# Third staging buffer, finer waits, and a router moved into the normalisation, in an eight-core transformer layer

## The chip, the cores and the metric

The kernel runs on 8 cores of one Trainium2 chip. All cores run one program; each computes 1024 tokens of one of two sequences of 4096, and reads 256 more on either side for the attention window (EXT = 1536 tokens). The cores don't exchange data. The metric is the device time of the slowest core, in microseconds (us).

## The reference, cut to what matters

```python
x = x + 0.5 * ffn(layernorm(x))          # x: (2, 4096, 4096) f32
x = x + attn(layernorm(x))
x = x + 0.5 * ffn(layernorm(x))

def ffn(x):                               # W_base 4096x4096, 8 experts of rank 16, top 2
    logits = x @ W_router.T
    p, idx = top_k(softmax(logits), 2); p = p / p.sum()
    combine = sum over k of p[k] * one_hot(idx[k])
    h = einsum('nd,erd->ner', x, A) * combine[:, :, None]
    return x @ W_base.T + b_base + 2 * einsum('ner,eor->no', h, B)

def attn(x):                              # 32 query heads of 128, one key and value head
    Q, K, V = x @ Wq.T, x @ Wk.T, x @ Wv.T
    Q, K = rope(Q), rope(K)
    for i in range(0, S, 256):            # windows of 512, half overlapping
        a = sigmoid(Q[i:i+512] @ K[i:i+512].T * scale); a = a / a.sum(-1)
        w = a @ V[i:i+512]
        out = linear blend of the former window's w and this one
    return out @ Wo.T
```

## The kernel before

Activations stand feature by token: `xlnb` holds the normalised input, 32 feature chunks x 1536 tokens, in bf16. Everything else on chip lives in one SBUF tensor, `arena`, carved up anew for each stage, so the profile names nearly every tile `arena`. The order of work is written out by hand: `Prog.emit` appends an instruction to one engine's list with the semaphore counts that it waits for, and each engine runs its list in order. All loads of weights and small tables go through SyncE's (SP's) queue, all loads and stores of activations through GpSimd's (POOL's).

Three stages follow each other: `ffn` on 1536 tokens, `attn`, `ffn` on 1024 tokens.

**`ln_prep` (lines 184 to 249)** opens each stage. Per chunk of 128 tokens it loads 2 MB in two DMAs into one of two buffers, casts and squares them on ScalarE (L207, L208), sums over features with 32 matmuls (L214), derives mean and inverse deviation on one partition on VectorE, with a square root on ScalarE (L231), spreads them by two matmuls (L237, L239), and applies them with two VectorE passes (L241, L245). The load of chunk i waits for the apply of chunk i-2.

**`ffn`.** After `ln_prep`, for each 512 tokens (three times in the first `ffn`, twice in the second) come 32 matmuls with the adapters' A (L325), 32 with the router (L331), a copy of the logits (L335), transposes (L340), the gates of the two best experts on VectorE and ScalarE (L343 to L381), four transposes back (L385), a copy (L388) and the product of gates and A's result (L391). I call this the router phase. Then the loop over 32 output chunks `of`: four slices of W_base (8 x 128 columns, 512 KB) are loaded and cast, and for each 512 tokens 32 matmuls (L422) and the adapters' B (L425) are done, evicted and stored.

**`make_stager` (lines 251 to 267)** loads and casts all weights. A load goes into one of two f32 buffers of `wstage` and waits for the cast that last read this buffer; ScalarE casts it to bf16 (L263). The DMA instruction itself is always line 47.

**`attn`.** Eight slices of Wk and eight of Wv (256 KB each) are staged, then K and V computed. While the first group of heads runs, POOL copies x1 to x2 in HBM in 64 pieces (the precopy). 32 heads run in four groups of eight (`hp`, and `hh` within one). `stage_wq(h)` stages eight slices of Wq. `feed(k)` issues the next k of the 64 matmuls of the coming head's Q projection (L576), 32 for each half of the tokens. Per head: rope on VectorE (L593 to L600), then ScalarE's list gets the eight casts for head h+1, then five windows, each with two score matmuls (L616), `feed(6)`, a sigmoid (L626), two more score matmuls (L631), `feed(6)`, a sigmoid (L637), the product with V (L646), `feed(4)`, and the blend by diagonal matrices (L653 to L681). A group's last head stages nothing. A group's first Q projection is issued as a whole, `feed(64)`, behind its own eight casts. After each group the Wo phase runs 32 turns of two staged slices of Wo, 2 x 8 matmuls (L708), two evictions on ScalarE (L716) and two DMAs that add to x2 in HBM (L45); an eviction waits until the adding DMA two before has landed.

The wait at the heart of `feed`, before:

```python
if j == 0:
    w = [("scalar", wqc[h]), ("vector", prep_v)] + list(extra_first)
```

`wqc[h]` is ScalarE's count after all eight casts.

Of the kernel before, what the change touches and what calls it, by code (L numbers as in the profile page):

```python
# [89 lines left out]
def build():  # L90
# [177 lines left out]
    def ffn(src_r, dst_r, ntok):  # L268
# [20 lines left out]
        prep_v, prep_t = pd["vector"], pd["tensor"]
        a = Arena(arena_t, PREP_B)  # L290
        wstage = [a.f32(8 * 128, (8, 128)), a.f32(8 * 128, (8, 128))]
        wb = [a.bf16(NIF * 128, (NIF, 128)), a.bf16(NIF * 128, (NIF, 128))]
        sl_sizes = []
        t0 = 0
        while t0 < ntok:
            n = min(512, ntok - t0)
            sl_sizes.append((t0, n))
            t0 += n
        slabs = [[a.f32(n) for (s0, n) in sl_sizes] for _ in range(2)]
        gxb = a.f32(512)  # L300
        lg = arena_t[0:8, a.alloc(512) + 0:a.off]
        ltm = a.f32(32, (4, 8))
        gate = a.f32(32, (4, 8))
        eq1 = a.f32(32, (4, 8))
        eq2 = a.f32(32, (4, 8))
        mskb = a.f32(32)
        m1c = a.f32(4)
        m2c = a.f32(4)
        p1c = a.f32(4)
        p2c = a.f32(4)  # L310
        stage = make_stager(wstage)
# [2 lines left out]
        hw_cnt = 0
        hw_hist = [0] * (NTS + 2)
        se_prev = 0
        sg_prev = 0
# [511 lines left out]
```

How the kernel before makes its waits and increments, by code:

```python
            def run(eng):  # L738
                hw = {}
                for fn, waits, inc, isem in pr.ops[e]:
                    for (we, wv) in waits:
                        if we == e:
                            continue
                        if wv > 0 and hw.get(we, -1) < wv:
                            eng.wait_ge(sems[we], wv)
                            hw[we] = wv
                    ins = fn(eng)
                    if inc:
                        ins.then_inc(sems[isem], inc)
                if e == "gpsimd":
                    for s, v in total_st.items():
                        if v:
                            eng.wait_ge(sems[s], v)
```

## Time and profile before

| what | us |
|---|---|
| median of 2 runs | 5023.42 (5001.85 to 5044.99) |
| the profiled execution | 4825.5 |
| its span, slowest core (core 3) | 4824.0 |
| spans of the eight cores | 4787.1 to 4824.0 |
| granted TensorE clock, eight cores | 0.818 to 0.825 |
| busy PE / DVE / ACT / POOL | 3083.9 / 994.4 / 1313.3 / 533.5 |

The profile is of one execution, on its slowest core. PE is TensorE's matmuls and PEld its weight loads, DVE is VectorE, ACT ScalarE, POOL GpSimd, SP SyncE. A row of the timeline gives the start and the length of an instruction (or of several in a row, "x32") and in brackets how long its engine was idle before it and what ended that. PEclk is the clock granted to TensorE as a share of 2.4 GHz; its two levels are 0.5 (1.2 GHz) and 1.0. The stages lie in the span as follows: first `ffn` to 1063 us (router phases from 289.7), normalisation of `attn` to 1312, K and V to 1414, the four groups of heads with their Wo phases to 4083, second `ffn` to the end.

### The profile page before, as it was taken

What the parts mean: (1) busy time and instruction counts of PE and PEld (TensorE: products, weight loads), DVE (VectorE), ACT (ScalarE), POOL (GpSimd) and SP (SyncE); (2) the same over time, 40 slices, a digit from 0 to 9 for tenths busy, and PEclk for the clock granted to TensorE, in tenths of its full rate; (3) what the DMA queues carried; (4) which work ended last, traced back from release to release, by engine and by line L of the source; (5) the groups of instructions that cost most, each with busy time, mean ns of one, the idle gap of its engine ahead of it and who ended that gap; (6) DMA issues with size and microseconds to landing.
All of it is one profiled execution on the core that took longest, in us unless ns stands there. A gap on an engine that the chain in (4) does not pass through costs nothing.

```text
span 4824.0 us, 40133 instructions; the slowest of 8 cores (4787.1 to 4824.0 us)
## 1 busy us (share of the span) xinstructions
PE 3083.9 (64%) x14804; PEld 1474.6 (31%) x14804; DVE 994.4 (21%) x1698; ACT 1313.3 (27%) x1657; POOL 533.5 (11%) x772
## 2 busy tenths in 40 slices
PE   1359999983265555656656566556566565249998
PEld 1224444432123332223332233322233322124443
DVE  2531111115512220012220022200122200441111
ACT  3322211213312222322223322223222232423222
POOL 0101111111011101200002100012000021101111
PEclk8679999996677777877868788878888687569999
DMA  4415556553343324741117711148411177327776
GB/s 107 119 36 159 172 167 178 170 150 101 104 137 111 111 81 92 141 91 44 35 32 143 142 49 36 35 83 147 94 43 35 30 143 155 106 57 206 218 211 182
DMA packets 647219, 537.33 MB, mean 111 GB/s; under 512 B 33905, under 2 KB 566642, under 8 KB 646770
## 3 DMA queue, kind: packets, MB, share of 16 engines
q1 hardware_dynamic: 556914, 283.07, 22.1%
q0 software_dynamic: 90112, 251.71, 21.8%
q8 instruction: 119, 1.95, 0.2%
q14 instruction: 74, 0.61, 0.1%
HBM read 408.85 MB, written 125.83 MB: 111 GB/s over the span
## 4 chain that ended last, share of the span: by engine, by line
PE 44%; DMA 27%; DVE 11%; ACT 10%; issue 5%; DVEq 1%; POOL 1%; SPq 1%; ACTq 0%; POOLq 0%
PE PS L422 14%; PE PS L576 9%; DMA arena<-wqT 6%; DMA x2h<-arena 6%; PE PS L708 5%; DMA arena<-woT 5%; DMA arena<-x2h 5%; ACT arena L263 4%; PE PS L646 3%; DMA out<-arena 3%; PE PS L673 2%; PE PS L631 2%; DVE arena L653 2%; DVE arena L664 2%; PE PS L677 2%
## 5 line engine op out<-in xcount | busy, mean ns | idle before, releaser
L422 PE MATMUL PS<-arena 128*128 128x512 bf16 x5120 | 1137.4, 380 | 25.5 <-ACT arena L263 18.9
L263 ACT ACTIVATE arena<-arena 128x512 bf16<-128x512 f32 (+1 forms) x784 | 582.8, 765 | 1173.6 <-PE PS L425 455.2
L708 PE MATMUL PS<-arena 128*128 128x512 bf16 x2048 | 585.7, 450 | 349.8 <-ACT arena L263 349.8
L576 PE MATMUL PS<-arena 128*128 128x512 bf16 x2048 | 560.4, 415 | 306.9 <-ACT arena L263 306.9
L422 PEld LDWEIGHTS PS<-arena 128*128 128x128 bf16 x5120 | 502.1, 98 | 635.3 <-issue 36.3
L45 POOL DMA_DIRECT2D x2h<-arena x256 | 217.2, 849 | 2108.9 <-ACT arena L716 1854.8
L708 PEld LDWEIGHTS PS<-arena 128*128 128x128 bf16 x2048 | 220.0, 111 | 714.8 <-issue 572.9
L576 PEld LDWEIGHTS PS<-arena 128*128 128x128 bf16 x2048 | 207.7, 105 | 562.3 <-issue 384.6
L653 DVE COPY arena<-PS 128x516 f32<-128x516 f32 (+1 forms) x160 | 94.2, 589 | 1155.8 <-PE PS L646 1155.8
L716 ACT ACTIVATE arena<-PS 128x512 f32<-128x512 f32 x256 | 152.9, 597 | 647.3 <-PE PS L708 441.3
L673 PE MATMUL PS<-arena 128*128 128x128 f32 x512 | 133.4, 350 | 231.2 <-DVE arena L668 231.2
L214 PE MATMUL PSM<-arena 128*1 128x256 bf16 x512 | 90.1, 358 | 288.3 <-ACT arena L208 288.3
L429 DVE TENSOR_SCALAR arena<-arena 128x512 f32<-128x512 f32 x160 | 77.1, 482 | 785.1 <-DMA arena<-xin 411.8
L681 ACT ACTIVATE arena<-PS 128x256 bf16<-128x256 f32 x128 | 49.2, 384 | 662.6 <-PE PS L677 662.6
L593 DVE TENSOR_TENSOR arena<-PS,arena 128x1024 f32<-128x1024 f32 x32 | 39.0, 1219 | 833.6 <-PE PS L576 833.6
L646 PE MATMUL PS<-arena 128*128 128x130 bf16 x2048 | 159.8, 234 | 48.1 <-ACT arena L637 45.8
L637 ACT ACTIVATE arena<-PS 128x1024 bf16<-128x1024 f32 (+1 forms) x160 | 136.6, 854 | 189.1 <-PE PS L631 189.1
L673 PEld LDWEIGHTS PS<-arena 128*128 128x128 f32 x512 | 97.2, 237 | 278.9 <-issue 278.9
L626 ACT ACTIVATE arena<-PS 128x1024 bf16<-128x1024 f32 (+1 forms) x160 | 135.9, 850 | 137.1 <-PE PS L616 134.4
L646 PEld LDWEIGHTS PS<-arena 128*128 128x128 bf16 x2048 | 135.9, 104 | 116.4 <-issue 111.2
L207 ACT ACTIVATE arena<-arena 128x4096 bf16<-128x4096 f32 x32 | 115.7, 3615 | 190.4 <-DMA arena<-x1h 92.7
L616 PE MATMUL PS<-arena 128*128 128x512 bf16 (+1 forms) x320 | 95.8, 388 | 102.7 <-DVE arena L600 102.7
(95 smaller groups left out, 2216.3 us busy)
## 6 DMA issues: line engine op xcount, KB each, us to landing
arena<-wbaseT SPq DMA_DIRECT2D x256, 512.0 KB, 5.7
x2h<-arena POOLq DMA_DIRECT2D x320, 256.0 KB, 4.6
arena<-wqT SPq DMA_DIRECT2D x256, 256.0 KB, 2.9
arena<-woT SPq DMA_DIRECT2D x256, 256.0 KB, 5.4
arena<-xin POOLq DMA_DIRECT2D x24, 1024.0 KB, 10.2
arena<-xin POOLq DMA_DIRECT2D x96, 256.0 KB, 3.9
x1h<-arena POOLq DMA_DIRECT2D x96, 256.0 KB, 2.3
arena<-x1h POOLq DMA_DIRECT2D x24, 1024.0 KB, 9.7
```

Of the source, the lines that this page charges most:

```text
L45: fn = lambda q, o=out, i=in_: q.dma_start(out=o, in_=i, accum_op=ALU.add)
L207: pr.emit("scalar", lambda s, p=par: s.activation(xb[p][:, :, 0:128], xf[p], ACT.Copy), wsc, 1)
L263: c = pr.emit("scalar", lambda s, si=i % 2, d=dst_bf_ap: s.activation(d, wstage[si], ACT.Copy), wc, 1)
L422: pr.emit("tensor", lambda t, c=c, sl=slot, of=of, t0=t0, n=n: t.matmul(sl, wb[of % 2][:, c, :], xlnb[:, c, t0:t0 + n], start=(c == 0), st ...
L576: qmm[h] = pr.emit("tensor", lambda t, c=c, par=h % 2, hf=hf: t.matmul(PS1[:, hf * 512:(hf + 1) * 512], wqb[par][:, c, :], xlnb[:, c, 256 ...
L626: pr.emit("scalar", lambda s, qn=qn, sp=sp: s.activation(sgb[sp][:, 0:2, 0:qn], PS2[:].rearrange("p (c t) -> p c t", c=2)[:, :, 0:qn], ACT ...
L637: sig_cnt = pr.emit("scalar", lambda s, qn=qn, sp=sp: s.activation(sgb[sp][:, 2:4, 0:qn], PS2[:].rearrange("p (c t) -> p c t", c=2)[:, :, ...
L646: avm = pr.emit("tensor", lambda t, p=p, kc=kc, kc0=kc0, st=st, sp_=sp_, sp=sp: t.matmul(PS3[:, p * 256:p * 256 + 130], sgb[sp][:, kc, p * ...
L653: wn_last = pr.emit("vector", lambda v, npp=npp, wi=wi: v.tensor_copy(wnr[wi % 2][:, 0:npp, :], PS3v[:, 0:npp, 0:129]), [("tensor", avm)], 1)
L673: pr.emit("tensor", lambda t, b=b, j=j, sA=sA: t.matmul(PS4[:, j * 128:(j + 1) * 128], wnr[b % 2][:, sA + j, 0:128], diag[:, j, :], start= ...
L708: mmc = pr.emit("tensor", lambda t, gg=gg, of=of, ts2=ts2, sl=slot: t.matmul(sl[:, 0:512], wqb[of % 2][:, gg, :], wout8[:, gg, ts2 * 512:( ...
L716: ev = pr.emit("scalar", lambda s, sli=sli, sl=slot: s.activation(slabs[sli], sl[:, 0:512], ACT.Copy), [("tensor", mmc), (xsem, pr.cnt[xse ...
```

## The change

Three edits. `make_stager` takes as many buffers as it is given, and is given three in `ffn` and in `attn`; the third has a DMA semaphore of its own. `feed` no longer waits for all eight casts at its first matmul: in the first half of the tokens, each fourth matmul waits for the cast of the slice that it and the next three read. The router phase of `ffn` becomes a function, `aphase`, called from a hook inside `ln_prep` after every fourth chunk's apply, on the 512 tokens that are then normalised. Its PSUM results move to halves of PS1 and PS2 that `ln_prep` doesn't use, and its small tiles to a place before `ln_prep`'s buffers.

```diff
-    def ln_prep(src_r, ntok, base, entry=()):
+    def ln_prep(src_r, ntok, base, entry=(), hook=None):
...
+            if hook is not None:
+                hook(i, apply2)
...
     def make_stager(wstage):
+        nb = len(wstage)
...
-            if i - 2 in state["cast"]:
-                wdma.append(("scalar", state["cast"][i - 2]))
-            sem = "wload%d" % (i % 2)
-            g = pr.dma(sem, wstage[i % 2], src_ap, wdma)
+            if i - nb in state["cast"]:
+                wdma.append(("scalar", state["cast"][i - nb]))
+            sem = "wload%d" % (i % nb)
+            g = pr.dma(sem, wstage[i % nb], src_ap, wdma)
...
-        pd = ln_prep(src_r, ntok, PREP_B, snap1)
...
-        for ts in range(NTS):
+        def aphase(ts, wait_v):
...
-            wmm = [("vector", prep_v)]
+            wmm = [("vector", wait_v), ("scalar", sm_cast)]
...
+        def hook(i, ap2):
+            if i % 4 == 3 and (i // 4) < NTS:
+                aphase(i // 4, ap2[i])
+
+        pd = ln_prep(src_r, ntok, OFL_B, snap1, hook=hook)
...
+        wstage = [a.f32(8 * 128, (8, 128)) for _ in range(3)]
...
-        wstage = [a.f32(4 * 128, (4, 128)), a.f32(4 * 128, (4, 128))]
+        wstage = [a.f32(4 * 128, (4, 128)) for _ in range(3)]
...
         def stage_wq(h, extra=()):
+            subs = []
...
-                stage(wqT_r[:, s8 * 4:(s8 + 1) * 4, h * 128:(h + 1) * 128],
-                      wqb[h % 2][:, s8 * 4:(s8 + 1) * 4, :], (), ew)
+                subs.append(stage(wqT_r[:, s8 * 4:(s8 + 1) * 4, h * 128:(h + 1) * 128],
+                            wqb[h % 2][:, s8 * 4:(s8 + 1) * 4, :], (), ew))
+            wq_sub[h] = subs
...
                     w = []
+                    if hf == 0 and c % 4 == 0:
+                        w.append(("scalar", wq_sub[h][c // 4]))
                     if j == 0:
-                        w = [("scalar", wqc[h]), ("vector", prep_v)] + list(extra_first)
+                        w += [("vector", prep_v)] + list(extra_first)
```

On ScalarE, in the normalisation of the first `ffn`, around the end of chunk 3, the order before is this (L231 is the square root of chunk 3, L207 and L208 cast and square chunk 4, then chunk 5):

```order
L231 ACTIVATE arena<-arena 1x128
L207 ACTIVATE arena<-arena 128x32x128
L208 ACTIVATE arena<-arena 128x32x128
L231 ACTIVATE arena<-arena 1x128
L207 ACTIVATE arena<-arena 128x32x128
```

Now at the same place (L325 is the copy of the logits, L335 that of the transposed logits, L350 and L353 the sigmoids, four pairs of them, L380 the copy of the gates; in the changed file):

```order
L231 ACTIVATE arena<-arena 1x128
L325 ACTIVATE arena<-PS 8x512
L335 ACTIVATE arena<-PS 128x32
L350 ACTIVATE arena<-arena 128x1
L353 ACTIVATE arena<-arena 128x1
...
L380 ACTIVATE arena<-PS 128x512
L207 ACTIVATE arena<-arena 128x32x128
L208 ACTIVATE arena<-arena 128x32x128
L231 ACTIVATE arena<-arena 1x128
```

The whole router phase stands between chunk 3's square root and chunk 4's cast. The same holds on TensorE and VectorE, after chunks 3, 7 and 11 of the first `ffn` and 3 and 7 of the second; the last hook is where the router's last phase stood before.

In `attn` no instruction changes its place; waits do. TensorE's list in window 0 of head 0, before (L616 and L631 are score matmuls, L576 the Q matmuls of the next head, L646 the product with V):

```order
L616 MATMUL PS<-arena 128x256 [waits s_vector]
L616 MATMUL PS<-arena 128x256
L576 MATMUL PS<-arena 128x512 [waits s_scalar]
L576 MATMUL PS<-arena 128x512 x5
L631 MATMUL PS<-arena 128x256 [waits s_scalar]
L631 MATMUL PS<-arena 128x256
L576 MATMUL PS<-arena 128x512 x6
```

And now (L634 and L649 are the score matmuls, L594 the Q matmuls, in the changed file):

```order
L634 MATMUL PS<-arena 128x256 [waits s_vector]
L634 MATMUL PS<-arena 128x256
L594 MATMUL PS<-arena 128x512 [waits s_scalar]
L594 MATMUL PS<-arena 128x512 x3
L594 MATMUL PS<-arena 128x512 [waits s_scalar]
L594 MATMUL PS<-arena 128x512
L649 MATMUL PS<-arena 128x256 [waits s_scalar]
L649 MATMUL PS<-arena 128x256
L594 MATMUL PS<-arena 128x512 x6
```

One wait for eight casts has become a wait for the first cast and, four matmuls later, one for the second; the later casts need no wait of their own here, since L649 waits for a sigmoid that stands behind all of them on ScalarE.

## Rows read from the trace of the kernel before

**Rows 1.** The page: its first line, and the chain that ended last, by line.
```profile
span 4824.0 us, 40133 instructions; the slowest of 8 cores (4787.1 to 4824.0 us)
...
PE PS L422 14%; PE PS L576 9%; DMA arena<-wqT 6%; DMA x2h<-arena 6%; PE PS L708 5%; DMA arena<-woT 5%; DMA arena<-x2h 5%; ACT arena L263 4%; PE PS L646 3%; DMA out<-arena 3%; PE PS L673 2%; PE PS L631 2%; DVE arena L653 2%; DVE arena L664 2%; PE PS L677 2%
```

**Rows 2.** Groups and waits of the whole span: us in total, times, longest us.
```profile
L263 ACT ACTIVATE arena<-arena 128x512 bf16<-128x512 f32 (+1 forms) x784 | 582.8, 765 | 1173.6 <-PE PS L425 455.2 <-DMA arena<-wbaseT 396.0 <-DMA arena<-wqT 277.5
...
PE PS L576 <- ACT arena L263: 306.9, 28, 17.3
...
ACT arena L716 <- DMA x2h<-arena: 206.0, 82, 4.3
```

**Rows 3.** Windows: length; busy PE, PEld, DVE, ACT, POOL; PEclk, DMA share, GB/s.
```profile
375.00:1063.00 688.00, 686.67 (x3168) 310.47 (x3166) 106.77 (x191) 127.72 (x124) 101.39 (x188) 1.00 0.58 167
1312.00:1352.00 40.00, 0.58 (x2) 0.28 (x3) 0.00 (x0) 10.07 (x16) 5.51 (x11) 0.50 0.71 216
1850.00:2084.00 234.00, 146.26 (x512) 54.81 (x510) 0.00 (x0) 70.62 (x126) 53.46 (x63) 0.85 0.76 142
2164.09:2181.16 17.07, 7.21 (x28) 2.97 (x29) 0.50 (x2) 4.86 (x8) 0.00 (x0) 0.54 0.40 115
2181.16:2189.46 8.30, 6.65 (x45) 3.62 (x44) 2.09 (x7) 2.05 (x2) 0.00 (x0) 1.00 0.00 0
```

**Rows 4.** Timeline, head 9: start us, us, instruction [idle before]; ScalarE, then TensorE.
```profile
2161.55 1.14 ACT L263 ACTIVATE arena<-arena 128x512 bf16<-128x512 f32 x2
...
2170.17 0.63 ACT L263 ACTIVATE arena<-arena 128x512 bf16<-128x512 f32 x1 [0.68 <-DMA arena<-wqT]
...
2173.76 0.63 ACT L263 ACTIVATE arena<-arena 128x512 bf16<-128x512 f32 x1 [0.68 <-DMA arena<-wqT]
...
2174.53 2.72 PE L576 MATMUL PS<-arena 128*128 128x512 bf16 x6 [9.86 <-ACT arena L263]
2177.05 0.63 PE L631 MATMUL PS<-arena 128*128 128x256 bf16 x2
```

**Rows 5.** Waits from 1430 to 1850 us, the first group of heads.
```profile
PE PS L576 <- ACT arena L263: 68.5, 6, 11.8
```

**Rows 6.** Timeline of ScalarE, head 2, beside the precopy.
```profile
1537.66 0.63 ACT L263 ACTIVATE arena<-arena 128x512 bf16<-128x512 f32 x1 [1.13 <-DMA arena<-wqT]
...
1541.60 0.63 ACT L263 ACTIVATE arena<-arena 128x512 bf16<-128x512 f32 x1 [1.57 <-DMA arena<-wqT]
```

**Rows 7.** Timeline, first head of the second group: ScalarE, then TensorE.
```profile
2084.34 1.14 ACT L263 ACTIVATE arena<-arena 128x512 bf16<-128x512 f32 x2
...
2094.67 0.63 ACT L263 ACTIVATE arena<-arena 128x512 bf16<-128x512 f32 x1 [1.43 <-DMA arena<-wqT]
...
2098.12 0.63 ACT L263 ACTIVATE arena<-arena 128x512 bf16<-128x512 f32 x1 [1.24 <-DMA arena<-wqT]
...
2098.89 16.75 PE L576 MATMUL PS<-arena 128*128 128x512 bf16 x64 [17.28 <-ACT arena L263]
```

**Rows 8.** Timeline, normalisation, chunks 3 to 5: VectorE, then ScalarE.
```profile
128.58 4.42 DVE L245 TENSOR_TENSOR arena<-arena,PS 128x4096 bf16<-128x4096 f32 x1
...
129.32 3.62 ACT L207 ACTIVATE arena<-arena 128x4096 bf16<-128x4096 f32 x1 [7.60 <-DMA arena<-xin]
...
144.56 0.31 ACT L231 ACTIVATE arena<-arena 1x128 f32<-1x128 f32 x1 [8.11 <-DVE arena L230]
145.74 3.62 ACT L207 ACTIVATE arena<-arena 128x4096 bf16<-128x4096 f32 x1 [0.87 <-DMA arena<-xin]
```

**Rows 9.** Timeline, the three router phases: TensorE, then ScalarE.
```profile
289.71 9.90 PE L325 MATMUL PS<-arena 128*128 128x512 bf16 x32 [9.19 <-DVE arena L245]
...
309.78 1.28 ACT L358 ACT_TABLE_LOAD   x1 [1.67 <-DVE arena L355]
...
316.92 0.60 ACT L388 ACTIVATE arena<-PS 128x512 f32<-128x512 f32 x1 [4.25 <-PE PS L385]
...
365.11 0.60 ACT L388 ACTIVATE arena<-PS 128x512 f32<-128x512 f32 x1 [4.25 <-PE PS L385]
```

More of the change, by code:

```diff
@@ L287, in ffn @@
         snap1 = [("scalar", sm_cast), ("vector", pr.cnt["vector"]), ("tensor", pr.cnt["tensor"])]
-        pd = ln_prep(src_r, ntok, PREP_B, snap1)
[L289 to L311, printed above, removed]
-        NTS = ntok // 512
[L314 to L317, printed above, removed]
-        for ts in range(NTS):
+        ga = Arena(arena_t, PREP_B)
+        gxb = ga.f32(512)
+        lg = arena_t[0:8, ga.alloc(512) + 0:ga.off]
+        ltm = ga.f32(32, (4, 8))
+        gate = ga.f32(32, (4, 8))
+        eq1 = ga.f32(32, (4, 8))
+        eq2 = ga.f32(32, (4, 8))
+        mskb = ga.f32(32)
+        m1c = ga.f32(4)
+        m2c = ga.f32(4)
+        p1c = ga.f32(4)
+        p2c = ga.f32(4)
+        OFL_B = ga.off
+        NTS = ntok // 512
+        st_aph = {"hw": 0, "hw_hist": [0] * (NTS + 2), "se": 0, "sg": 0}
+        def aphase(ts, wait_v):
             cols = slice(ts * 512, (ts + 1) * 512)
             hslot = PS3[:, (ts % 2) * 512:(ts % 2) * 512 + 512]
-            wmm = [("vector", prep_v)]
+            wmm = [("vector", wait_v), ("scalar", sm_cast)]
             if ts >= 2:
-                wmm.append(("vector", hw_hist[ts - 2]))
+                wmm.append(("vector", st_aph["hw_hist"][ts - 2]))
             for c in range(NIF):
@@ L331, in ffn @@
                 h_cnt = pr.emit("tensor", lambda t, c=c, cc=cols: t.matmul(
[L332 removed]
+                    PS1[0:8, 512:1024], rb16[:, c, :], xlnb[:, c, cc],
                     start=(c == 0), stop=(c == NIF - 1)), wrt if c == 0 else [],
                     1 if c == NIF - 1 else 0)
[L335 removed]
+            se = pr.emit("scalar", lambda s: s.activation(lg, PS1[0:8, 512:1024], ACT.Copy),
                          [("tensor", h_cnt)], 1)
[L337 removed]
+            st_aph["se"] = se
             tp = 0
@@ L385, in ffn @@
                 tg = pr.emit("tensor", lambda t, qc=qc: t.transpose(
-                    PS4[:, qc * 128:(qc + 1) * 128], gxb[:, qc * 128:(qc + 1) * 128], id32),
+                    PS2[:, 512 + qc * 128:512 + (qc + 1) * 128], gxb[:, qc * 128:(qc + 1) * 128], id32),
                     [("vector", vgx), ("scalar", se2)] if qc == 0 else [], 1 if qc == 3 else 0)
-            sg = pr.emit("scalar", lambda s: s.activation(gxb, PS4[:, 0:512], ACT.Copy),
+            sg = pr.emit("scalar", lambda s: s.activation(gxb, PS2[:, 512:1024], ACT.Copy),
                          [("tensor", tg)], 1)
-            sg_prev = sg
-            hw_hist[ts] = hw_cnt = pr.emit("vector", lambda v, h=hslot, cc=cols: v.tensor_tensor(
-                hwb[:, cc], h, gxb, ALU.mult), [("scalar", sg)], 1)
+            st_aph["sg"] = sg
+            st_aph["hw_hist"][ts] = st_aph["hw"] = pr.emit(
+                "vector", lambda v, h=hslot, cc=cols: v.tensor_tensor(
+                    hwb[:, cc], h, gxb, ALU.mult), [("scalar", sg)], 1)
+        def hook(i, ap2):
+            if i % 4 == 3 and (i // 4) < NTS:
+                aphase(i // 4, ap2[i])
+        pd = ln_prep(src_r, ntok, OFL_B, snap1, hook=hook)
+        prep_v, prep_t = pd["vector"], pd["tensor"]
+        hw_cnt = st_aph["hw"]
+        a = Arena(arena_t, OFL_B)
+        wstage = [a.f32(8 * 128, (8, 128)) for _ in range(3)]
+        wb = [a.bf16(NIF * 128, (NIF, 128)), a.bf16(NIF * 128, (NIF, 128))]
+        sl_sizes = []
+        t0 = 0
+        while t0 < ntok:
+            n = min(512, ntok - t0)
+            sl_sizes.append((t0, n))
+            t0 += n
+        slabs = [[a.f32(n) for (s0, n) in sl_sizes] for _ in range(2)]
+        stage = make_stager(wstage)
         grp_cnt = {}
@@ L546, in attn @@
         dg_guard = 0
+        wq_sub = {}
         def stage_wq(h, extra=()):
+            subs = []
             for s8 in range(8):
```

17 lines of the change are left out of this document (8 added, 9 removed).

## The prediction

> **What bounds the kernel now.** I read the page's chain of waits first [rows 1]. No engine owns it: TensorE's two large products (L422, the feed-forward; L576, the Q projection) lead, and then come loads of weights (wqT, woT) and stores. So each stage has its own limit, and I read them one at a time.
>
> The waits and groups show where engines stand still [rows 2]. TensorE waits 306.9 us, in 28 pieces, ahead of L576, for ScalarE's L263, the cast of a weight slice from f32 to bf16. L263 itself waits 277.5 us for wqT, 396.0 for wbaseT and 455.2 for TensorE. These three are 1128.7 of its 1173.6 us, which leaves 45 us for all other loads: woT costs hardly any wait. In the Wo stretches the evictions L716 wait for accumulating stores instead (206.0 us).
>
> The windows give the limits [rows 3]. The first feed-forward's product loop, 375 to 1063 us, has TensorE busy 686.67 of 688 us at full clock: a third staging buffer gives nothing there. The K/V staging (1312 to 1352) has TensorE idle, the DMA engines 0.71 busy. In the Wo phase (1850 to 2084) they are 0.76 busy. In one head of the attention, 17.07 us lie between the first score matmul of window 0 and that of window 1, at a mean clock of 0.54, half level (1.2 GHz) nearly throughout; the next window takes 8.30 us at full level (2.4 GHz).
>
> The cause is in the timeline of that head [rows 4]. ScalarE casts eight slices for the next head before its first sigmoid: two at once, then each as its load lands, from 2161.55 to 2174.39 us, 12.8 us for 8 x 0.63 = 5.0 us of work. With two buffers a load starts only when the cast two before is done. TensorE stands still for 9.86 us, because the first L576 matmul waits for all eight casts, and its six matmuls of 0.427 us then stand before L631. The counts [rows 5] say six such stops in the first group of heads, so 24 in four groups; the other four of the 28 are at the groups' first heads.
>
> **The change part by part, against the profiled execution (4825.5 us, its span 4824.0).**
>
> *Third buffer in the heads.* The load of slice i now waits for cast i-3. Casts 0 to 2 run at once, and the loads that fed casts 2 to 5 at present now feed 3 to 6 at the same times; one more, triggered by cast 2, joins them. So cast 7 comes about where cast 5 stands today, 2170.17 instead of 2173.76: 3.6 us [rows 4]. In the first group of heads, where a precopy shares the DMA engines, it is 1541.60 - 1537.66 = 3.9 us [rows 6]. Bounds: nothing, if three loads in flight land no sooner than two; and 7.8 us, if all waits between casts go (12.8 - 5.0).
>
> *The Q matmuls wait by quarter-slices.* The first six need casts 0 and 1 alone, so they run while ScalarE still casts. Today they occupy TensorE from 2174.53, and L631 starts at 2177.05 [rows 4]. It would otherwise start when the sigmoid has ended, some 0.8 us after 2174.30, so 2.0 us go. Against that, window 1 is reached sooner after TensorE's restart and may begin at the lower level: between 0 and 0.8 us, I take 0.4. Per head: 3.6 + 2.0 - 0.4 = 5.2, and 5.5 in the first group. Heads: 18 x 5.2 + 6 x 5.5 = 126.6 us.
>
> *First head of each group.* Today 64 matmuls wait for eight casts: casts from 2084.34 to 2098.75, matmuls from 2098.89 for 16.75 us, to 2115.64 [rows 7]. By the same rule cast 7 comes at 2094.67 and ends at 2095.30; 28 matmuls are done by then, and 36 x 0.216 = 7.8 us remain: 2103.1, so 12.5 us earlier. If TensorE stayed at 1.2 GHz for all 64 (27.3 us from 2085.2) only 3.1 us would be won; with matmuls queued nearly all the time I take 12.5. Four times: 50.0.
>
> *K and V staging.* Sixteen slices in the 40 us of that window. The DMA engines' own work is 0.71 x 40 = 28.4, so at most 11 us can go, at least none. I take 8, nearer the upper end, since each cast there waits for a load.
>
> *Wo phases.* Loads of woT are issued at the same casts as today and are already hidden [rows 2]: 0. *Feed-forward loops:* 0, as read above; at their start three slices instead of two are there when the gates end, which saves one step from landing to landing. Two such steps are 3.6 us in rows 4, so I take 1.8, between none and 3.6: 3.6 together.
>
> *The router moved into the normalisation.* This one costs. The hook puts 64 matmuls and the gate chain behind chunks 3, 7 (and 11), on every engine in program order, ScalarE's included. Chunk 4's L207 today starts at 129.32, 3.7 us before chunk 3 is applied (128.58 + 4.42 = 133.00) [rows 8]. Now it stands behind the gate copy, which in today's first phase ends 27.8 us after the phase's first matmul begins (289.71 to 316.92 + 0.60 [rows 9]), 28.0 with the semaphore behind the apply: 31.7 us late. Chunk 5 follows behind chunk 4's square root (144.56 + 0.31 - 129.32 = 15.6 us later) and a table load of 1.3 us [rows 9], at 44.9 instead of 12.7 after the apply (145.74 - 133.00): 32.2 late. Chunk 7 hangs on chunk 5, through the buffer. So a hook in the middle costs 32.2 us, three times (two in the first feed-forward, one in the second): 96.6. At the end one phase is left where there were three, and two: a later phase costs (365.11 - 316.92) / 2 = 24.1 us [rows 9], three times 72.3. Net +24.3 us. Its loads on POOL and SP wait for the applies as before, so only order counts. Bounds: -72 if the hooks were hidden wholly, +97 if the end gave nothing back.
>
> The load of the sigmoid table takes 1.28 us [rows 9], and six more changes of table come in, all counted above. The Trainium skill (ScalarE: Activation LUTs, "What ACT_TABLE_LOAD costs") gives 2.66 us for a change, with a drain; the row shows 1.28, and no run here shows the rest. By the page the sum would be 8 us worse.
>
> Sum: -126.6 - 50.0 - 8.0 - 3.6 + 24.3 = -163.9 us, that is 4661.6 in the profiled execution, 3.4% less. The median of the two runs shown, 5023.42, is 4.1% above the profiled one (factor 1.041), for a reason that the profile does not show. I scale with it: -170.6, 4853 us.
>
> **The rivals.**
>
> *TensorE wakes earlier.* Window 0 runs at a mean clock of 0.54, window 1 at 1.00 [rows 3]. If the matmuls run during the casts bring the full level forward, the rest of window 0 is some 2.0 us shorter and the 0.4 is not lost: 24 x 2.4 = 57.6 more; 163.9 + 57.6 = 221.5, x 1.041 = 231, 4793 us. For it: the idle piece of 9.86 us [rows 4] shrinks by the cast gain and the 2.6 us of the six matmuls, to under 4. Against: only six matmuls are let in. The Trainium skill (TensorE: Matmul & The Clock Gate, "HAM oscillation — how this bites in real kernels") says that a product interrupted by waits for its next slice falls to half clock each time, and that this goes when the waits go. The 0.54 agrees with the first half; the second would give this rival.
>
> *Three loads land no sooner.* Then the casts stay as they are; only the quarter waits gain: 24 x 1.6 = 38.4 in heads, at a group's first head 2098.75 + 7.8 = 2106.6, so 9.1 x 4 = 36.4, less 24.3: 50.5, x 1.041 = 52.6, 4971 us. Against: the DMA engines are 0.40 busy in that stretch [rows 3], so a third load in flight has room.
>
> *Slower: the accumulating stores.* The Wo phase has 4 x 32 = 128 turns, each bound in part by a landing [rows 2], with the DMA engines 0.76 busy [rows 3]. If deeper staging delays each landing by x, it costs 128 x: from 1.28 us on the whole gain is gone. At 2.2 us it is 281.6 - 163.9 = +117.7, x 1.041, 5146 us. Against: the same loads are issued at the same casts.
>
> *The hook does hide the router,* as its place suggests. Then -72.3 instead of +24.3: 163.9 + 96.6 = 260.5, x 1.041 = 271, 4752 us. Against: ScalarE's order, above.
>
> **How the numbers follow.** Forecast 4853: 0.54. Earlier clock 4793: 0.23. No sooner 4971: 0.12. Slower: 0.04. Hidden router: 0.04. The rest, 0.03, are sums of small misses. A measurement here tells 2% from nothing: faster by more than that is below 4923. Forecast, clock, hidden router and some of the rest give 0.84 faster, 0.12 same, 0.04 slower. The range is 4650 to 4930. Its low end takes in the sum against the profiled execution itself (4662), should the runs of the changed kernel lie there; its high end holds the forecast with the bad ends of K/V, first heads and feed-forward starts (8 + 38 + 4), and a margin for a quarter of the cast gain in the heads. It leaves out the two cases above.
>
> **What would show it.** Right: between score matmuls of windows 0 and 1 some 11.5 instead of 17.07 us; the wait L576 for casts down from 306.9 to under 120; wqT's waits at least a third less; first head's Q matmuls end some 19 us after the casts began, not 31; chunk 4's L207 some 28 us after chunk 3's apply instead of 3.7 before it; six more table loads; Wo phases unchanged near 233 us. Wrong: the eighth cast still 12 us after the first; that L207 within 10 us of the apply; Wo phases longer by over 10 us each; or a window 1 at half clock.

## The result and the profile after

The changed kernel takes 0.9717 of the time of the kernel before, with a 95% interval of 0.9689 to 0.9745: 2.8% faster, where the forecast's sum was 3.4%. Its profiled execution took 4678.3 us, and the median of its 11 runs is 4702.99 us. Runs of both kernels lie near the profiled time or some 4% above it, and the ratio compares the near ones alone; the factor 1.041 in the forecast of 4853 us came from two runs that were both of the far ones. The range, 4650 to 4930, holds the median.

The page's first line and its chain by line:

```profile
span 4676.8 us, 40189 instructions; the slowest of 8 cores (4646.6 to 4676.8 us)
...
PE PS L434 24%; DMA x2h<-arena 8%; PE PS L594 8%; PE PS L726 6%; DMA arena<-wqT 4%; ACT arena L266 4%; PE PS L664 3%; DMA arena<-woT 3%; PE PS L691 2%; PE PS L649 2%; DVE arena L671 2%; ACT arena L207 2%; ACT arena L208 2%; DVE arena L682 2%; PE PS L695 2%
```

The chain of [rows 1] had wqT at 6% and the Q matmuls (L576, now L594) at 9%; they are down to 4% and 8%. The product loop (L422, now L434) leads by more than before, 24%. Groups, table loads and waits of the whole span (us in total, times, longest us):

```profile
L266 ACT ACTIVATE arena<-arena 128x512 bf16<-128x512 f32 (+1 forms) x784 | 567.5, 762 | 1052.1 <-PE PS L437 612.3 <-DMA arena<-wbaseT 232.9 <-DMA arena<-wqT 168.8
...
L594 PE MATMUL PS<-arena 128*128 128x512 bf16 x2048 | 579.3, 425 | 18.1 <-ACT arena L266 16.9 <-DVE arena L533 1.1
...
L350 ACT ACT_TABLE_LOAD x5 | 6.4, 1283 | 8.3 <-DVE arena L347 8.3
L231 ACT ACT_TABLE_LOAD x5 | 6.4, 1283 | 38.6 <-DVE arena L230 38.6
...
ACT arena L734 <- DMA x2h<-arena: 222.4, 92, 4.5
...
PE PS L649 <- ACT arena L644: 157.9, 73, 7.0
```

Against [rows 2], TensorE's wait for casts ahead of the Q matmuls went from 306.9 to 16.9 us, and ScalarE's wait for wqT from 277.5 to 168.8. Part of it moved: the second pair of score matmuls (L649, before L631) now waits 157.9 us for the first sigmoid, where it waited 47.1 before (below), since in window 0 no Q matmuls cover that wait any longer. Together the two waits fell from 354.0 to 174.8 us. From the kernel before:

```profile
PE PS L631 <- ACT arena L626: 47.1, 49, 1.3
```

The wait of the Wo evictions for accumulating stores stays (222.4, before 206.0). There are ten table loads at L231 and L350, six more than before.

Windows, columns as in [rows 3]:

```profile
387.98:1074.00 686.02, 686.02 (x3167) 310.41 (x3168) 106.07 (x190) 124.45 (x124) 101.39 (x188) 1.00 0.56 167
1327.00:1361.00 34.00, 0.00 (x0) 0.00 (x0) 0.00 (x0) 10.07 (x16) 4.36 (x8) 0.50 0.84 234
1813.46:2050.00 236.54, 148.61 (x512) 55.59 (x512) 0.00 (x0) 70.29 (x127) 53.46 (x63) 0.84 0.77 140
2165.59:2178.30 12.71, 8.59 (x29) 3.67 (x30) 0.60 (x2) 4.23 (x7) 0.00 (x0) 0.50 0.51 146
2178.30:2186.60 8.30, 6.66 (x46) 3.62 (x45) 1.99 (x6) 2.05 (x2) 0.00 (x0) 1.00 0.00 0
```

The product loop is unchanged, 686 us at full clock. K/V staging has the DMA engines 0.84 busy instead of 0.71. One Wo phase: 236.5 us, 0.77 busy. Window 0 of head 10 takes 12.71 us, where head 9 took 17.07 before, and all of it at the lower level, 0.50. Over 24 heads the mean went from 16.8 to 12.5 us. Window 1 runs at the full level, 8.30 us at 1.00, as before. The timeline of that head, ScalarE, then TensorE:

```profile
2162.58 1.66 ACT L266 ACTIVATE arena<-arena 128x512 bf16<-128x512 f32 x3
...
2171.60 0.63 ACT L266 ACTIVATE arena<-arena 128x512 bf16<-128x512 f32 x1 [0.93 <-DMA arena<-wqT]
2172.14 0.58 ACT L644 ACTIVATE arena<-PS 128x512 bf16<-128x512 f32 x1
...
2165.97 2.76 PE L594 MATMUL PS<-arena 128*128 128x512 bf16 x6
2172.86 0.59 PE L649 MATMUL PS<-arena 128*128 128x256 bf16 x2 [4.12 <-ACT arena L644]
2173.24 2.77 PE L594 MATMUL PS<-arena 128*128 128x512 bf16 x6
2175.80 1.08 PE L664 MATMUL PS<-arena 128*128 128x130 bf16 x8
2176.66 1.80 PE L594 MATMUL PS<-arena 128*128 128x512 bf16 x4
2178.30 0.60 PE L634 MATMUL PS<-arena 128*128 128x512 bf16 x2
```

Three casts at once and the last at 2171.60 us: 9.65 us from first to last, not 12.8 [rows 4]. Six Q matmuls run in that time. TensorE then idles until 2172.86, and everything behind it runs at half clock: six Q matmuls at 0.427 us each, the product with V (L664, 1.08 us for 8), four more in 1.80 us. Before, the same stretch read as follows (TensorE, head 9, behind the last of [rows 4]):

```profile
2177.48 2.53 PE L576 MATMUL PS<-arena 128*128 128x512 bf16 x6
2179.84 0.62 PE L646 MATMUL PS<-arena 128*128 128x130 bf16 x8
2180.30 1.02 PE L576 MATMUL PS<-arena 128*128 128x512 bf16 x4
```

There TensorE restarted with the first six Q matmuls at 2174.53, and at 2179.84 the full level was back, while window 0 still ran: L646 took 0.62 us and the four 1.02. Here it restarts only with L649 at 2172.86, nearer to the end of window 0 (2178.30), and the full level comes with window 1. So in these two heads 1.08 - 0.62 + 1.80 - 1.02 = 1.24 us of the gain are given back.

The first head of the second group, ScalarE, then TensorE:

```profile
2049.89 1.66 ACT L266 ACTIVATE arena<-arena 128x512 bf16<-128x512 f32 x3
...
2063.93 0.63 ACT L266 ACTIVATE arena<-arena 128x512 bf16<-128x512 f32 x1 [1.35 <-DMA arena<-wqT]
...
2061.29 7.93 PE L594 MATMUL PS<-arena 128*128 128x512 bf16 x36 [0.78 <-ACT arena L266]
```

The casts run from 2049.89 to 2064.56, the matmuls between them; the last 36 matmuls go in 7.93 us, at full clock, and end at 2069.22, 19.3 us after the first cast began, where [rows 7] show 31.3.

The normalisation around the first hook (VectorE, ScalarE, and VectorE again, chunk 7):

```profile
127.36 4.42 DVE L245 TENSOR_TENSOR arena<-arena,PS 128x4096 bf16<-128x4096 f32 x1
...
158.81 0.60 ACT L380 ACTIVATE arena<-PS 128x512 f32<-128x512 f32 x1 [4.24 <-PE PS L377]
159.30 3.61 ACT L207 ACTIVATE arena<-arena 128x4096 bf16<-128x4096 f32 x1
...
174.49 1.28 ACT L231 ACT_TABLE_LOAD   x1 [8.07 <-DVE arena L230]
175.78 0.31 ACT L231 ACTIVATE arena<-arena 1x128 f32<-1x128 f32 x1
...
239.54 4.42 DVE L245 TENSOR_TENSOR arena<-arena,PS 128x4096 bf16<-128x4096 f32 x1
```

Chunk 4's L207 starts at 159.30, 27.5 us after chunk 3's apply ended (131.78), where [rows 8] had it 3.7 us before. Directly ahead of it stands L380, the gate copy. Then a table load. Chunk 7's apply ends 112.2 us after chunk 3's.

### Where the time went

All eight cores run one program without exchange, so I cut each core's trace at the same instructions and took the median over eight cores. The heads are counted from one rope's first instruction to the next's; the 24 are those that hold a cast row before window 0. In us, and beside it the same for the experiments below. A few matmul records of cores 0 and 6 are missing, so the stretches are cut by time and not by counting. Not listed are the first product loop (685.3 and 686.2) and small stretches, and medians don't add exactly, so the columns don't add up to the span. e1 is its first trace. The router's delay is the last row but one: the time from chunk 3's apply to chunk 7's.

| stretch | before | after | e1 | e2 | e3 | e4 | e5 | e6 | e8 | e9 | e10 |
|---|---|---|---|---|---|---|---|---|---|---|---|
| 24 heads | 1246.5 | 1148.2 | 1146.9 | 1155.4 | 1239.1 | 1257.3 | 987.2 | 1145.0 | 984.1 | 1099.4 | 985.4 |
| last eviction to rope, 3 groups | 94.9 | 60.2 | 61.3 | 84.3 | 72.5 | 94.1 | 61.3 | 61.1 | 60.3 | 61.0 | 61.9 |
| first K matmul to first rope | 78.5 | 66.4 | 66.2 | 74.5 | 72.3 | 78.3 | 65.6 | 65.8 | 66.1 | 65.7 | 65.2 |
| K/V staging | 41.0 | 34.4 | 34.7 | 34.5 | 41.8 | 41.8 | 34.7 | 34.4 | 34.5 | 34.6 | 34.5 |
| first opening, to first product matmul | 371.7 | 384.9 | 368.3 | 365.5 | 366.6 | 386.4 | 369.2 | 322.7 | 322.2 | 385.6 | 323.9 |
| second opening | 261.3 | 269.7 | 258.2 | 258.8 | 260.8 | 269.1 | 259.1 | 241.7 | 241.6 | 266.4 | 243.0 |
| Wo phases, 4 | 928.8 | 932.7 | 934.7 | 934.5 | 936.9 | 930.1 | 937.1 | 935.8 | 940.8 | 933.4 | 944.5 |
| last heads of groups, 4 | 204.1 | 201.2 | 200.6 | 204.1 | 200.9 | 204.1 | 204.1 | 200.5 | 203.2 | 200.5 | 178.1 |
| second product loop | 461.2 | 458.0 | 477.9 | 462.8 | 466.7 | 460.3 | 461.4 | 464.3 | 458.1 | 474.8 | 465.2 |
| chunk 3 to chunk 7 (within the first opening) | 78.7 | 110.0 | 78.0 | 76.7 | 77.0 | 110.2 | 78.2 | 77.3 | 77.6 | 110.1 | 79.0 |
| span | 4802.4 | 4671.0 | 4661.8 | 4688.1 | 4786.9 | 4837.6 | 4500.8 | 4594.9 | 4442.7 | 4640.0 | 4414.2 |

### The profile page after: what moved, and what is told of

Same layout as the page of the kernel before. It is cut to its first block, busy times and chain, and to the rows that moved or that the text cites. A ratio compares the mean times of both kernels' runs of the same rounds, so it can differ in the third digit from the quotient of the medians.

```text
span 4676.8 us, 40189 instructions; the slowest of 8 cores (4646.6 to 4676.8 us)
## 1 busy us (share of the span) xinstructions
PE 3111.3 (67%) x14804; PEld 1482.2 (32%) x14804; DVE 994.3 (21%) x1698; ACT 1303.9 (28%) x1663; POOL 533.3 (11%) x772
## 4 chain that ended last, share of the span: by engine, by line
PE 54%; DMA 19%; DVE 10%; ACT 10%; issue 5%; DVEq 1%; SPq 1%; POOL 0%; ACTq 0%; POOLq 0%
PE PS L434 24%; DMA x2h<-arena 8%; PE PS L594 8%; PE PS L726 6%; DMA arena<-wqT 4%; ACT arena L266 4%; PE PS L664 3%; DMA arena<-woT 3%; PE PS L691 2%; PE PS L649 2%; DVE arena L671 2%; ACT arena L207 2%; ACT arena L208 2%; DVE arena L682 2%; PE PS L695 2%
## 5 line engine op out<-in xcount | busy, mean ns | idle before, releaser
L434 PE MATMUL PS<-arena 128*128 128x512 bf16 x5120 | 1135.9, 380 | 15.2 <-ACT arena L266 15.2
L266 ACT ACTIVATE arena<-arena 128x512 bf16<-128x512 f32 (+1 forms) x784 | 567.5, 762 | 1052.1 <-PE PS L437 612.3
L434 PEld LDWEIGHTS PS<-arena 128*128 128x128 bf16 x5120 | 501.9, 98 | 623.2 <-issue 22.3
L594 PE MATMUL PS<-arena 128*128 128x512 bf16 x2048 | 579.3, 425 | 18.1 <-ACT arena L266 16.9
L726 PEld LDWEIGHTS PS<-arena 128*128 128x128 bf16 x2048 | 220.7, 112 | 717.4 <-issue 575.9
L594 PEld LDWEIGHTS PS<-arena 128*128 128x128 bf16 x2048 | 213.4, 107 | 273.4 <-issue 98.8
L649 PE MATMUL PS<-arena 128*128 128x512 bf16 (+1 forms) x320 | 95.7, 388 | 158.0 <-ACT arena L644 157.9
L664 PE MATMUL PS<-arena 128*128 128x130 bf16 x2048 | 167.0, 240 | 49.0 <-ACT arena L655 45.8
L664 PEld LDWEIGHTS PS<-arena 128*128 128x128 bf16 x2048 | 142.7, 108 | 123.2 <-issue 122.3
L634 PE MATMUL PS<-arena 128*128 128x512 bf16 (+1 forms) x320 | 96.0, 388 | 106.8 <-DVE arena L618 106.8
```

The lines of the kernel that those rows point to most:

```text
L266: c = pr.emit("scalar", lambda s, si=i % nb, d=dst_bf_ap: s.activation(d, wstage[si], ACT.Copy), wc, 1)
L434: pr.emit("tensor", lambda t, c=c, sl=slot, of=of, t0=t0, n=n: t.matmul(sl, wb[of % 2][:, c, :], xlnb[:, c, t0:t0 + n], start=(c == 0), st ...
L594: qmm[h] = pr.emit("tensor", lambda t, c=c, par=h % 2, hf=hf: t.matmul(PS1[:, hf * 512:(hf + 1) * 512], wqb[par][:, c, :], xlnb[:, c, 256 ...
L649: s23 = pr.emit("tensor", lambda t, kc=kc, q0w=q0w, qn=qn, kc0=kc0, par=par: t.matmul(PS2[:, (kc - 2) * 512:(kc - 2) * 512 + qn], krb[:, ( ...
L664: avm = pr.emit("tensor", lambda t, p=p, kc=kc, kc0=kc0, st=st, sp_=sp_, sp=sp: t.matmul(PS3[:, p * 256:p * 256 + 130], sgb[sp][:, kc, p * ...
L726: mmc = pr.emit("tensor", lambda t, gg=gg, of=of, ts2=ts2, sl=slot: t.matmul(sl[:, 0:512], wqb[of % 2][:, gg, :], wout8[:, gg, ts2 * 512:( ...
```

## The experiments

Theory A: the gain is all in the attention, and the hook costs, since it is one serial piece on ScalarE. Rivals: the hook gives part of the gain; the loads or the waits alone give it.

### e1: the router back behind the normalisation

```diff
-        pd = ln_prep(src_r, ntok, OFL_B, snap1, hook=hook)
+        pd = ln_prep(src_r, ntok, OFL_B, snap1)
...
+        for ts in range(NTS):
+            aphase(ts, prep_v)
```

> The changed kernel with its router phases put back behind the normalisation; third buffer and finer waits stay. Theory A (the hook is serial on ScalarE and costs more than it saves, the gain is all in the attention): the two feed-forward openings are 13 and 8 us shorter than in the changed kernel, as before; ratio to the kernel before 0.967, the changed kernel being at 0.972. Rival (the hook hides the router and part of the gain came from it): ratio 0.985 or more.

Its four runs gave no interval. The second timing, of eight:

> Third buffer and finer waits, router behind the normalisation, timed again for its interval. Theory A: ratio 0.967. Rival (the hook cost nothing that the time shows): 0.972.

0.9681 (0.9639 to 0.9722). The times alone don't part it from the changed kernel's 0.9717, since the intervals overlap. The traces do: the two openings are 16.6 and 11.5 us shorter than in the changed kernel (368.3 and 258.2 against 384.9 and 269.7), and the 24 heads are as there (1146.9 and 1148.2). The span is only 9.2 us shorter, since the second product loop, the same in both, took 19.9 us more. The rival is out: without the hook nothing of the gain is missing. The hook costs 28.1 us by this comparison, 7 more than the 21 stated.

### e2: the third buffer alone

The router as in e1, and `feed` waits for all eight casts again:

```diff
-                    if hf == 0 and c % 4 == 0:
-                        w.append(("scalar", wq_sub[h][c // 4]))
                     if j == 0:
-                        w += [("vector", prep_v)] + list(extra_first)
+                        w += [("scalar", wqc[h]), ("vector", prep_v)] + list(extra_first)
```

> Only the third staging buffer; the first Q matmul waits for all eight casts again, router behind the normalisation. Theory A: 3.2 us less per cast window in 24 heads (77), about 3.5 us at 4 first heads (14), 6 us at K and V, a few at the ends: about 100 us less, ratio 0.979; the six Q matmuls stand again before L631's counterpart. Rival (three loads in flight gain nothing, the finer waits did it): ratio 0.995 or more.

0.9716 (0.9663 to 0.9768): as fast as the whole change, by a third buffer alone. The span of its traces says 4688.1 / 4802.4 = 0.976, within that interval. Theory A's 0.979 lies just above it, the rival's 0.995 far. In the heads it won 91.1 us, 3.8 each. TensorE in head 10:

```profile
2166.85 2.72 PE L594 MATMUL PS<-arena 128*128 128x512 bf16 x6 [6.29 <-ACT arena L266]
...
2169.79 1.95 PE L594 MATMUL PS<-arena 128*128 128x512 bf16 x6
2171.57 0.62 PE L664 MATMUL PS<-arena 128*128 128x130 bf16 x8
```

The six Q matmuls stand ahead of L649, as before. But the full level comes back during the second six (1.95 us for six, where the changed kernel takes 2.77), and L664 takes 0.62 us: this row of matmuls, which only delays the scores, pays for itself in part through the clock.

### e3: the finer waits alone

Both `wstage` lists with two buffers, the router as in e1.

> Only the waits by quarter-slices, with two buffers, router behind the normalisation. Theory A as predicted: 4 x 9 us at first heads and 1.6 us in each of 24 heads, 75 us, ratio 0.985. Theory A corrected by the trace after (the restart at half clock takes most of the 2 us back): 0.7 us a head, 53 us, ratio 0.989. Rival (waits change nothing in heads, loads decide): 36 us, 0.993.

0.9918 (0.9878 to 0.9958), less than 1% faster; the median span says 0.997. The first heads of groups gain (94.9 to 72.5, 78.5 to 72.3), the 24 heads only 7.4 us, 0.3 each. Predicted were 1.6. The corrected theory stated 0.7 a head, still too much; the rival, nothing in heads, is nearer. Third buffer and finer waits together (e1) give 99.6 in the heads, 8.5 more than the buffer alone.

### e4: the hook alone

Two buffers and the wait of e2, the hook as in the change.

> Only the router phases moved into the normalisation, two buffers, the wait for all eight casts. Theory A: slower by 22 to 27 us, ratio 1.005, the applies of chunks 3 and 7 some 111 us apart instead of 79. Rival (hook hides the router): faster by 72 us, ratio 0.985.

1.0038 (1.0001 to 1.0074), slower, by its times hardly clear of noise; the traces say +14.7 and +7.8 us at the openings, 22.5 in all, against the kernel before. Against e3, which also has two buffers and no hook, it is 28.1, as between the changed kernel and e1. Chunks 3 and 7 are 110.2 us apart, 78.7 before. The hook hides nothing.

### e5: casts a head ahead

If eight casts in one row are what is left, spreading them should remove it. wqb of head h+2 is free throughout head h.

```diff
                 if hh < 7:
-                    stage_wq(h + 1)
+                    if hh == 0:
+                        stage_wq(h + 1)
...
                     sig2_prev = sig_cnt
+                    if hh < 6 and wi >= 1:
+                        stage_wq(h + 2, part=range(2 * wi - 2, 2 * wi))
```

> Router behind the normalisation, third buffer, finer waits; and the casts for head h+2 stand in windows 1 to 4 of head h, two each behind the second sigmoid, instead of eight for head h+1 ahead of window 0. Theory A (the remaining cost of staging in a head is that eight casts stand in one row on ScalarE while TensorE idles and restarts at half clock): window 0 falls from 12.1 to about 6.5 us as in the group's first head, 24 heads from 1147 to about 1000 us, ratio 0.935. Rival (loads or ScalarE are then late in windows 1 to 4, or TensorE's clock stays low): heads above 1100 us, ratio 0.955 or more.

0.9335 (0.9308 to 0.9362), as theory A said. Head 10:

```profile
2090.69 0.59 PE L636 MATMUL PS<-arena 128*128 128x256 bf16 x2 [2.91 <-DVE arena L619]
...
2091.38 0.60 ACT L646 ACTIVATE arena<-PS 128x512 bf16<-128x512 f32 x1 [3.12 <-PE PS L636]
...
2097.05 0.59 PE L636 MATMUL PS<-arena 128*128 128x512 bf16 x2
...
2100.51 1.14 ACT L266 ACTIVATE arena<-arena 128x512 bf16<-128x512 f32 x2
```

The sigmoid follows the scores by 0.69 us, window 0 takes 6.4, and the casts stand in pairs where ScalarE idled. The 24 heads fell to 987.2 us, from 1146.9 in e1.

### e6: the router in steps

`aphase` becomes a generator that stops at eleven places. `ln_prep` calls it where the engine of the next step would idle; the step runs if its name fits, so at most one row of matmuls a chunk. The five calls of a chunk stand behind L208, the statistics' matmuls, the square root, the spreading matmuls and the apply.

```diff
+            tick(i, "act1", apply2)
+            tick(i, "pe1", apply2)
+            tick(i, "act2", apply2)    
+            tick(i, "pe2", apply2)
+            tick(i, "end", apply2)
...
+            yield "pe2"
             for c in range(NIF):
```

> The changed kernel with each router phase cut into steps that stand at points of the following chunks where the engine they run on would idle (32 matmuls behind a chunk's spread, copies behind its squares, gates behind its apply), instead of as one piece. Theory A (the hook costs because it is one serial piece in ScalarE's order, not because there is no room): T3 to T7 back to 79 to 84 us, first opening from 385 to about 320 us, second from 270 to about 240, ratio 0.950 to 0.955. Rival (the normalisation has no room for 64 matmuls and the gates): openings above 360 and 258 us, ratio 0.967 or more.

0.9531 (0.9499 to 0.9563), theory A's number. TensorE in chunks 4 to 6, then ScalarE (L320 and L327 are the adapters' and the router's matmuls, L216 the statistics, L332 the copy of the logits):

```profile
139.45 8.54 PE L320 MATMUL PS<-arena 128*128 128x512 bf16 x31 [0.16 <-issue]
147.93 3.73 PE L216 MATMUL PS<-arena 128*1 128x256 bf16 x32
...
155.87 8.76 PE L327 MATMUL PS<-arena 128*8 128x512 bf16 x32
...
163.62 3.60 ACT L209 ACTIVATE arena<-arena 128x4096 bf16<-128x4096 f32 x1
167.12 0.57 ACT L332 ACTIVATE arena<-PS 8x512 f32<-8x512 f32 x1
```

Both rows of 32 matmuls fill what was idle, and L332 stands behind L209 and waits for nothing. Chunks 3 and 7 are 77.3 us apart. The openings fell to 322.7 and 241.7 us, 62 and 28 below the changed kernel. So the router can be hidden under the normalisation; the place of the hook was not enough, the order within it decided.

### e7: twelve matmuls before the sigmoid

```diff
-                    feed(6)
+                    early = 12 if (wi == 0 and 1 <= hh <= 6) else 6
+                    feed(early)
...
-                    feed(6)
+                    feed(12 - early)
```

> The changed kernel; in window 0 of the 24 heads twelve Q matmuls stand ahead of the first sigmoid's scores and none behind them, instead of six and six. Theory B (after the restart TensorE runs at half clock and the six matmuls behind the sigmoid hold up the product with V): window 0 from 12.1 to about 10.8 us, 25 to 40 us less in all, ratio 0.965. Rival (TensorE's time in window 0 is hidden behind ScalarE): window 0 unchanged, ratio 0.972.

0.9705 (0.9677 to 0.9733): no difference from the change can be told, and 0.965 is excluded. But its trace shows that theory B came true in window 0 and was paid back in window 1. Means over the 24 heads on cores 4, 5 and 7 (their windows 2 and 3 take 8.2 us, as in every kernel here): window 0 fell from 12.6 to 11.6 us, window 1 grew from 8.4 to 9.25, and the head is left 0.2 us shorter. One head on core 7, windows 0 and 1, columns as in [rows 3], then TensorE (L650 stands for L649, L665 for L664):

```profile
2144.97:2156.74 11.77, 7.92 (x29) 3.30 (x29) 0.59 (x2) 4.23 (x7) 0.00 (x0) 0.64 0.60 166
2156.74:2166.01 9.27, 7.63 (x45) 3.99 (x44) 1.99 (x6) 2.05 (x2) 0.00 (x0) 0.88 0.00 0
```

```profile
2145.35 4.43 PE L594 MATMUL PS<-arena 128*128 128x512 bf16 x12
2152.79 0.59 PE L650 MATMUL PS<-arena 128*128 128x256 bf16 x2 [3.01 <-ACT arena L645]
2154.21 1.02 PE L665 MATMUL PS<-arena 128*128 128x130 bf16 x8 [0.84 <-ACT arena L656]
```

Twelve matmuls in 4.43 us are faster than half level allows (six take 2.77 in the changed kernel), so the full level came while they ran. After 3.01 us of idling L665 again takes 1.02 us instead of 0.62: the level had fallen. Window 1 then has a mean clock of 0.88 where it had 1.00, its first matmuls still at half level. So the forecast's price for an early window 1 exists; it shows here and not in the change itself.

### e9: filling the idle piece

e3 had left open why six matmuls out of the way give so little. The rows of window 0 above suggest the clock (theory C). The test adds work that gives nothing but occupation:

```diff
+        def idle_mm(n):
+            for _ in range(n):
+                pr.emit("tensor", lambda t: t.matmul(
+                    PSM[:, 0:512], krb[:, 0:128], xlnb[:, 0, 0:512], start=True, stop=True), [], 0)
...
                     feed(6)
+                    if wi == 0 and 1 <= hh <= 6:
+                        idle_mm(9)
```

> The changed kernel with nine matmuls that nobody reads (into a free PSUM bank) behind the first six Q matmuls of window 0 in 24 heads, where TensorE now idles about 4 us until the casts end. Theory C (what the finer waits give is taken back because TensorE restarts at half clock after that idle piece): the second half of window 0 runs at full clock, window 0 falls from 12.1 to about 10.5 us, 24 heads from 1148 to about 1110, ratio 0.964. Rival (the clock does not bind there, ScalarE does): window 0 stays at 12 us or grows, ratio 0.972 or more.

0.9634 (0.9586 to 0.9682), and 24 heads from 1148.2 to 1099.4 us, 2.0 each. TensorE in head 10 (L605 is the filling, L656 stands for L649):

```profile
2142.37 3.22 PE L605 MATMUL PSM<-arena 128*128 128x512 bf16 x9
2146.96 0.38 PE L656 MATMUL PS<-arena 128*128 128x256 bf16 x2 [1.37 <-ACT arena L651]
...
2148.47 0.62 PE L671 MATMUL PS<-arena 128*128 128x130 bf16 x8
```

and its windows, columns as in [rows 3]:

```profile
2139.43:2146.96 7.53, 5.94 (x17) 2.25 (x19) 0.00 (x0) 3.64 (x6) 0.00 (x0) 0.66 0.73 201
2146.96:2149.79 2.83, 2.83 (x21) 1.62 (x21) 0.51 (x2) 0.60 (x1) 0.00 (x0) 1.00 0.55 154
```

All nine fit in the idle piece. From the sigmoid on, all runs at full clock: 2.83 us from L656 to the next window, where the changed kernel needs 5.44 (2172.86 to 2178.30). ScalarE's row of casts is as long as before (a mean of 9.8 us in both). So the rival falls: the clock does bind here. It is the 2 us of the prediction, with the clock's part put back in: against e2, which has the third buffer alone, the head is 2.3 us shorter.

### e8 and e10: both together, and filling the last heads

> Casts a head ahead and the router in steps together. Theory A: both gains add, ratio 0.915 to 0.925. Rival: what one gains the other loses, ratio 0.94 or more.

> Casts a head ahead and router in steps, timed again for its interval. Theory A (both gains add): 0.9335 less 0.9717 - 0.9531 = 0.0186, less the hook's own 0.004 to 0.005 that the first has not: about 0.919 to 0.920. Rival: 0.93 or more.

Neither timing gave an interval. The lowest times are 4450.4 and 4464.6 us, then 4458.2 and 4460.5; the lowest of the kernel before, beside them, are 4832.7 and 4827.4, so the lowest against the lowest is 0.921 and 0.924. The stretches add as stated: 984.1 us in the heads as in e5, openings as in e6. The rival, 0.93 or more, doesn't fit.

e10 adds `idle_mm(k)` for the missing `feed(k)` in each group's last head:

> Casts a head ahead, router in steps, and in each group's last head, which has no Q matmuls of a next head, sixteen matmuls a window that nobody reads. Theory C (that head runs its windows at half clock for want of work, 10.8 us each instead of 8.2): its 50 us fall to about 42, four times, from 203 to about 170 us; ratio 0.006 to 0.008 below casts ahead and router in steps without them. Rival (the clock costs nothing on that chain): 203 us stay.

0.9189 (0.9151 to 0.9227): 8.1% less than the kernel before. Against e8 the times alone don't tell it (lowest 4441.5 and 4450.4 us); the median spans do, 4414.2 against 4442.7. The four last heads fell from 203.2 to 178.1 us, 25 instead of the 33 stated. Window 1 of head 15 without the filling (e8), then window 1 with it (e10), columns as in [rows 3]:

```profile
2248.45:2259.32 10.87, 5.80 (x28) 3.75 (x28) 2.46 (x8) 2.17 (x3) 0.00 (x0) 0.50 0.00 0
```

```profile
2276.91:2285.21 8.30, 6.65 (x45) 3.62 (x44) 2.08 (x7) 2.05 (x2) 0.00 (x0) 1.00 0.00 0
```

The same chain of work, 10.87 us at 0.50 and 8.30 us at 1.00.

Once the heads are short, something else comes up. The first of the four Wo phases grew: from 232 us (median) before to 248 in e10. Its evictions wait for the precopy's last store, which the first group of heads no longer outlasts. ScalarE in e10, core 3 (L768 is the eviction): it is idle for 16.73 us ahead of the first one, where it was 3.87 in the kernel before, and the precopy's last store was issued at 1704.00:

```profile
1706.44 1.09 ACT L768 ACTIVATE arena<-PS 128x512 f32<-128x512 f32 x2 [16.73 <-DMA x2h<-arena]
```

## Why the prediction was right, and where its terms were off

The verdict held, and the way: faster, out of the attention, less a loss in the feed-forward. By terms, forecast against the table (median of cores):

- *Third buffer in the heads,* 3.6 and 3.9 us each, 88 in all: 91.1 (e2). Right, and so was the rule that cast 7 comes where cast 5 stood, nearly: 9.65 us for the row where 9.25 was reckoned, with loads of wqT that now take 3.3 us to land, not 2.9 (medians).
- *"So 2.0 us go"*, the six Q matmuls out of the way, less 0.4 for the clock: this step failed, in its price for the clock. The 1.6 left of it gave 0.3 a head with two buffers (e3) and 0.35 with three (e1 against e2). 24 x 1.25 = 30 us, nearly the whole of the miss (163.9 forecast, 131.4 measured). The 2.0 themselves came: from the end of the last cast to the second pair of score matmuls it is 2.66 us in e2 and 0.63 in e1 (means over 24 heads on the six cores with complete records). But from there to window 1 it is 3.44 us in e2 and 4.90 in e1: 1.46 are given back, where I had put 0.4. Another 0.1 to 0.2 goes in a longer row of casts and in the windows behind. With two buffers it is the same, 3.55 against 4.95. I had put the clock's price into window 1, because I read 0.54 in window 0 as "half level nearly throughout". In fact the last 1.3 us of window 0 ran at full level already, and that was lost. e9 shows that it is the clock: filled, the stretch takes 3.01 us instead of 4.80, with the same row of casts ahead of it.
- *First heads,* 12.5 us, four times 50.0: 34.7 at three groups and 12.1 at the first head of all, 46.8. Right.
- *K and V,* 8: 6.6. *The hook, and starts,* +24.3 - 3.6 = +20.7: +13.2 and +8.4, together 21.6. Right in its mechanism (e1, e4, e6): chunks 3 and 7 come 31.3 us further apart, 32.2 forecast. That the sum agrees within 1 us is in part luck, since the openings of the kernels without the hook range from 365.5 to 371.7 us: the hook costs 22.5 us by e4 against the kernel before, and 28.1 by e4 against e3 or by the changed kernel against e1, where I had 24.3. The starts are as forecast: from the last apply to the first product matmul three buffers save 1.7 and 1.6 us (e1 against e3). Six more table loads of 1.283 us, as counted.
- *Wo phases and product loops,* 0: +3.9 and -3.2 here. The Wo phases are +5.7 in e2 with the third buffer alone, but +8.1 in e3 with two, so no effect of the buffer shows; the loops of the second feed-forward range from 458 to 478 us over kernels that are the same there.

The absolute forecast, 4853 us, missed the median by 150 us, and it did so through the factor 1.041 and not through the sum: without the factor it was 4661.6, for a profiled execution that took 4678.3. The range held the median because its low end was set for that case.

The rival of the earlier clock had the right place and the wrong sign: the clock decided the size of the waits' term, but six matmuls don't bring the full level forward; twelve do, and lose it again in the idle piece behind them (e7); six and nine more, which leave 1.37 us of idling, do and keep it (e9). The stores' rival did not come: 4 us in four Wo phases, where it had 281.6. Nor did the hidden router, with this hook; with the steps of e6 it does, 49.0 + 19.6 = 68.6 us below the kernel before, where the rival said 72.3. Loads in threes do land later each (3.3 against 2.9 us), but the rival in which that eats the gain is refuted by e2.

Still open: why the openings without the hook differ by up to 6 us between kernels that hardly differ there, and whether e10's filling changes the time by more than its spans say, since e8 has no interval.

## What to carry to other kernels

When an engine's program is in order, hiding a phase is a matter of which instruction stands behind which: a piece put "in the middle" as a whole stops everything behind it, and the same instructions cut up and set where each engine idles cost next to nothing here (chunks 3 and 7 are 77.3 us apart in e6, 78.7 before). Count for a staging loop the casts that stand in one row ahead of the next needed result; one more buffer shortens the row, but issuing them a step ahead removes it (here 3.8 us a head for the buffer, and 6.7 more for issuing ahead). And before a saved wait is priced, read at which clock TensorE runs behind it: a shorter idle piece can leave the work behind it at half clock (here 1.46 of 2.0 us saved went back).
